# Reordering the steps of a two-layer attention pipeline on VectorE, GpSimd and the DMA queue

## The reference

```
x = x + tanh(g_xattn[0]) * L0_xattn(layernorm(x), ctx, ctx)     # similarity of probabilities, MLP of 1024 with gelu
x = x + tanh(g_ffn[0])   * L0_ffn(layernorm(x))                 # 256x256 product of values rounded to fp8
x = x + tanh(g_xattn[1]) * L1_xattn(layernorm(x), ctx, ctx, mask)   # 16 heads of 16, softmax
x = x + tanh(g_ffn[1])   * L1_ffn(layernorm(x))                 # dequantised weights, MLP of 1024 with silu
```

## Time and profile before

| what | us |
|---|---|
| median of 3 runs | 1618.51 |
| lowest and highest | 1613.52, 1624.93 |
| span of the profiled execution (first to last instruction) | 1614.4 |
| first stage and setup, up to the first instruction of the pipeline | 611 |

### The profile page before, as it was taken

The page is one execution under the profiler, slowest core; times in us unless marked ns, Lnnn a source line. Parts: engine busy times, 40 slices in busy tenths (PEclk is TensorE's granted clock), DMA queues, the critical chain, the costliest instruction groups (busy, mean ns, idle before and its releaser), DMA issues.

```text
span 1614.4 us, 42641 instructions
## 1 busy us (share of the span) xinstructions
PE 1486.5 (92%) x14155; PEld 1144.6 (71%) x14155; DVE 1316.4 (82%) x3187; ACT 1135.2 (70%) x2057; POOL 1034.7 (64%) x1392
## 2 busy tenths in 40 slices
PE   4999999999999972668999999999999999999997
PEld 2788888888888861435667676777777776777666
DVE  4698888888888875778988889898988889898742
ACT  7798888888888742355666666666666666676664
POOL 4588888888888744224556565665656566565445
PEclk9999999999999995588999999999999999999999
DMA  7322222322222002332223232232223232232200
GB/s 228 96 80 66 91 72 65 96 66 69 93 65 71 2 1 92 80 119 73 80 80 87 73 85 80 85 87 81 83 78 92 72 91 74 86 85 84 64 16 22
DMA packets 197690, 125.45 MB, mean 78 GB/s; under 512 B 44400, under 2 KB 196848, under 8 KB 197360
## 3 DMA queue, kind: packets, MB, share of 16 engines
q1 hardware_dynamic: 197616, 124.48, 26.2%
HBM read 92.69 MB, written 25.17 MB: 73 GB/s over the span
## 4 chain that ended last, share of the span: by engine, by line
PE 48%; SPq 4%; DVE 3%; issue 2%; DMA 2%; POOL 2%; ACT 1%; POOLq 0%
PE b_bank L1835 28%; PE b_bank L1910 7%; PE b_scoreT L1892 4%; PE b_score L1875 4%; PE b_bank L1843 2%; PE b_bank L1987 1%; SPq L1306 1%; DMA b_nmT<-b_nm 1%; DMA b_yT<-b_y 1%; SPq L1290 1%; DVE b_nm L1653 1%; SPq L1279 1%; PE b_bank L1925 1%; ACT b_E L1471 1%; SPq L1315 0%
## 5 line engine op out<-in xcount | busy, mean ns | idle before, releaser
L1471 ACT ACTIVATE b_E<-b_scoreT 128x1024 f32<-128x1024 f32 x256 | 262.2, 1024 | 152.5 <-PE b_scoreT L1892 151.3
L1653 DVE TENSOR_REDUCE b_nm<-b_score 128x4 bf16<-128x1024 f32 x256 | 313.3, 1224 | 54.6 <-PE b_score L1875 48.4
L31 ACT ACT_TABLE_LOAD x157 | 201.4, 1283 | 18.6 <-PEq L1059 15.2
L1835 PE MATMUL b_bank<-f,b_YT 128*128 128x256 bf16 x1536 | 190.3, 274 | 4.7 <-POOL b_YT L1404 4.6
L890 PE MATMUL bank<-hT,W1T 128*128 128x256 bf16 x1536 | 183.3, 273 | 2.4 <-DVE hT L706 1.7
L1835 PE MATMUL b_bank<-b_hT,f 128*128 128x256 bf16 x1536 | 183.4, 273 | 0.8 <-DVE X L1749 0.8
L890 PE MATMUL bank<-W2T,G 128*128 128x256 bf16 x1024 | 171.0, 272 | 6.7 <-DVE GT L780 6.2
L1835 PEld LDWEIGHTS b_bank<-f,b_YT 128*128 128x128 bf16 x1536 | 143.5, 98 | 39.7 <-issue 19.5
L1835 PEld LDWEIGHTS b_bank<-b_hT,f 128*128 128x128 bf16 x1536 | 147.7, 98 | 30.3 <-issue 12.6
L890 PEld LDWEIGHTS bank<-hT,W1T 128*128 128x128 bf16 x1536 | 148.0, 98 | 27.7 <-ACT G L549 4.0
L1388 POOL TENSOR_TENSOR b_v<-b_v,b_e 128x512 f32<-128x512 f32 x32 | 40.6, 1269 | 195.0 <-DVE b_e L1734 195.0
(11 more groups left out here) (222 smaller groups left out, 3524.8 us busy)
## 6 DMA issues: line engine op xcount, KB each, us to landing
b_Q<-q_dram SPq DMA_DIRECT2D x192, 64.0 KB, 2.6
b_K<-k_dram SPq DMA_DIRECT2D x192, 64.0 KB, 2.8
xin<-in_x SPq DMA_DIRECT2D x32, 256.0 KB, 3.2
ctxn<-in_ctx SPq DMA_DIRECT2D x32, 256.0 KB, 2.8
mask_in<-in_mask SPq DMA_DIRECT2D x32, 256.0 KB, 3.0
X<-in_x SPq DMA_DIRECT2D x32, 256.0 KB, 4.0
ctxt<-in_ctxT SPq DMA_DIRECT2D x32, 256.0 KB, 4.2
b_ctxt<-in_ctxT SPq DMA_DIRECT2D x32, 256.0 KB, 2.8
```

What stands on the lines that cost most here:

```text
L31: act.add_instruction(mybir.InstLoadActFuncSet(name=nc.get_next_instruction_name(), act_func_set_id=which, ins=[], outs=[]))
L1471: nc.scalar.activation(E[:, pair:pair + 2], scoreT_ps[:, :, :, :], ACT.Exp).then_inc(sig["E"], 1)
L1653: nc.vector.tensor_reduce(pair, score_ps[:, :, :, :], AX.X, ALU.max, negate=True).then_inc(sig["nm"], 1)
L1835: last = nc.tensor.matmul(out_tile, lhs(i, k), rhs(j, k), start=start and k == chunks[0] and (i, j) == TERMS[0], stop=stop and k == chunks ...
```

## The change

No instruction is added or removed; eight calls change place.

- VectorE: `scaled(n)` moves from the start of the iteration to just ahead of `binades(n)`. `statistics_2(f)` moves from behind `result` to ahead of `maxima(5)`. `mlp_normalised` moves from the start of an iteration to behind `maxima(6)` of the iteration before (so its batch is `o`, not `h`). `mask_bias` stays at its place but works one batch earlier (`q`, not `m`).
- GpSimd: `inverse_std_2(f)` comes before `silu_parts(h, 0)`, not after it; so both inverse deviations stand together.
- SyncE: `load_mask` comes before the spills and stacks, right behind `transpose_rounded`, and not behind `transpose_maxima`.

```diff
@@ -1327,14 +1327,13 @@
                     load_context()
                     transpose_rounded()
                 if q:
+                    load_mask()
                     spill_queries()
                     spill_keys()
                     stack_queries()
                     stack_keys()
                 if m:
                     transpose_maxima()
-                if q:
-                    load_mask()
                 if m:
                     row_of_maxima()
                 if w:
@@ -1440,11 +1439,10 @@
                     rounded()
                 if o:
                     inverse_std_3()
-                if h:
-                    silu_parts(h, 0)
                 if f:
                     inverse_std_2()
                 if h:
+                    silu_parts(h, 0)
                     silu_parts(h, 1)
                 if f:
                     context_parts()
@@ -1620,18 +1618,18 @@
                     nc.vector.tensor_tensor(xT[:, 1], whole_bank(BANK["xT"]), xT[:, 0], ALU.subtract).then_inc(sig["xlo"], 1)
 
                 def mask_bias():
-                    dve.wait_ge(sig[f"mask{m.parity}"], landed(m))
-                    if (due := done(m, back=2, per=NP)) is not None:
+                    dve.wait_ge(sig[f"mask{q.parity}"], landed(q))
+                    if (due := done(q, back=2, per=NP)) is not None:
                         dve.wait_ge(sig["scoreT_mm"], due)
-                    nc.vector.tensor_scalar(mb[m.parity][:, :, :], mask_in[:, :, :], 0.0, MINUS, ALU.is_equal,
+                    nc.vector.tensor_scalar(mb[q.parity][:, :, :], mask_in[:, :, :], 0.0, MINUS, ALU.is_equal,
                                             ALU.mult).then_inc(sig["mb"], 1)
 
                 def mlp_normalised():
-                    dve.wait_ge(sig["rs3"], done(h))
-                    if (due := done(h, back=1)) is not None:
+                    dve.wait_ge(sig["rs3"], done(o))
+                    if (due := done(o, back=1)) is not None:
                         dve.wait_ge(sig["hT_mm"], due)
                     for t in range(T):
-                        last = nc.vector.tensor_scalar(hn[:, t, :], Xb(h, t), mv3[:, t, 0:1], rh3[:, t:t + 1], ALU.subtract,
+                        last = nc.vector.tensor_scalar(hn[:, t, :], Xb(o, t), mv3[:, t, 0:1], rh3[:, t:t + 1], ALU.subtract,
                                                        ALU.mult)
                     last.then_inc(sig["hn"], 1)
 
@@ -1755,10 +1753,6 @@
 
                     dve.wait_ge(sig["b1_mm"], 1)
                     nc.vector.tensor_tensor(b1f[:, :], second["b1_raw"][:, :], b1_ps, ALU.add).then_inc(sig["b1f"], 1)
-                if h:
-                    mlp_normalised()
-                if n:
-                    scaled()
                 if o:
                     attended(0)
                 if m:
@@ -1782,6 +1776,7 @@
                 if h:
                     mlp_columns()
                 if n:
+                    scaled()
                     binades()
                 if f:
                     quantised_update()
@@ -1795,15 +1790,18 @@
                     keys_low()
                 if o:
                     attention_update()
+                if f:
+                    statistics_2()
                 if m:
                     maxima(5)
                     maxima(6)
+                if o:
+                    mlp_normalised()
                 if w:
                     result()
-                if f:
-                    statistics_2()
-                if m:
+                if q:
                     mask_bias()
+                if m:
                     maxima(7)
                 if f:
                     attention_normalised()
```

More of the change, by code:

```diff
@@ L1800, in iteration @@
                     maxima(6)
+                if o:
+                    mlp_normalised()
                 if w:
                     result()
-                if f:
-                    statistics_2()
+                if q:
+                    mask_bias()
                 if m:
-                    mask_bias()
                     maxima(7)
```

## The result

The changed kernel takes 1646.41 us (median of 4 runs, 1644.15 to 1652.79), the kernel before in the same comparison 1617.62: ratio 1.0177, 95% interval 1.0146 to 1.0208. It is slower, by 28.8 us; forecast were 26.5 us more and a median of 1645 us. The profiled execution has a span of 1644.8 us, 30.4 more than before.

The account below looks back on a forecast made before the run. TensorE, full from iteration 7 or 8, was taken as the bound, waiting on VectorE's chain at `scores(6)`. 30 - 3.5 + 0 = 26.5 us on the median of 1618.5 gave 1645 us, range 1633 to 1663.

Parts of the forecast that it names:

- 0.455 us to spare: Mean slack of VectorE's closed chain from `maxima(3)` to `maxima(5)`: 0.39 us in iteration 18, 0.52 in 17.
- the wait at `scores(6)`: TensorE waits there for `maxima(5)`: 1.33 us in iterations like 18, 1.20 in those like 17.
- The statistics: `statistics_2`, moved ahead of `maxima(5)`, adds 0.95 us to VectorE's chain; ends 0.95 and 1.01.
- The scaling: `scaled`, moved ahead of `binades`, adds 0.77 us to VectorE's chain; ends 0.65 and 1.06.
- Per iteration: Each steady iteration of the second stage, 7 to 31, gets 1.2 us longer.
- What came back: Iterations 8 to 14: the new delay gives DMA transfers more time, regaining 3.5 us; ends 0 and 4.
- The two waits for `b_on`: At `mlp_transposed`: of 5.29 us in iteration 6, 1.7 go; the 1.87 in iteration 7 go whole.
- The term of the start: Iterations 0 to 6: gains and losses sum to 0, give or take 4 us.
- the steady term: Iterations 7 to 31: 25 x 1.2 = 30 us more; ends 27 and 39.
- A (absorbed): Rival: the wait at `scores(6)` is absorbed, true slack 1.7 us; 1613 us, within 1%; chance 10%.
- B: Rival: faster by over 1%, as the start or the transfers win much more than is lost; chance 4%.
- C (the clock): Rival: TensorE's clock falls after the new wait, 32 us on top over 25 iterations, 1677 us; chance 5%.

Follow-up runs that it names:

- E6: Kernel before with one extra unused `bn_stats` on VectorE ahead of `maxima(4)`: 1617.97 us, ratio 1.0003.
- E7: Kernel before with four extra unused `bn_stats` on VectorE ahead of `maxima(4)`: 1641.19 us, ratio 1.0150.
- E8: Changed kernel with six extra unused `bn_stats` at the start of VectorE's iteration, ahead of `attended(0)`: 1651.49 us, ratio 1.0221 to the kernel before.
- E1: Kernel before with only `statistics_2` moved ahead of `maxima(5)`: 1627.6 us, ratio 1.0059.
- E2: Kernel before with only `scaled` moved to just ahead of `binades`: 1620.86 us, ratio 1.0017.
- E3: Changed kernel with `scaled` and `statistics_2` back in their old places: 1614.25 us, ratio 0.9986 to the kernel before.
- E12: Changed kernel with `scaled` and `binades` behind `quantised_update` instead of ahead of it: 1653.72 us, measured once.
- E4: As E3, but with `statistics_2` between `maxima(5)` and `maxima(6)`: 1613.7 us, ratio 0.9970 to the kernel before.

## Why the prediction was right

**The bound, and the place of the loss.** TensorE full, one score buffer, and a chain on VectorE from `maxima(3)` to `maxima(5)` with 0.455 us to spare: the wait at `scores(6)` appeared as forecast (1.20 us on the weight load, 0.92 between matmuls), at `scores(5)` as well (0.21 us between matmuls, in every second iteration), and nowhere else of weight. E6 and E7 show the slack, E8 that time ahead of the chain is worth nothing there, and the 0.44 us that E1 and E2 lack together show that both used the same slack.

One reading was a little off: VectorE did have idle time in the chain, 0.16 us in even iterations, in which the second instruction of `quantised_update` waits for the first. In odd ones that gap is 0.04 us, which is where the two values of the slack come from (kernel before, iterations 17 and 18):

```profile
1060.02 0.87 DVE L1658 SCALAR_TENSOR_TENSOR b_ob<-b_bank,scale_qk,fb_all 128x256 bf16<-128x256 f32 x2
...
1060.93 0.75 DVE L1662 SCALAR_TENSOR_TENSOR X<-b_ob,gate,X 128x512 bf16 x1
...
1087.96 0.87 DVE L1658 SCALAR_TENSOR_TENSOR b_ob<-b_bank,scale_qk,fb_all 128x256 bf16<-128x256 f32 x2
...
1088.98 0.75 DVE L1662 SCALAR_TENSOR_TENSOR X<-b_ob,gate,X 128x512 bf16 x1 [0.16 <-DVE b_ob L1658]
```

It costs the argument nothing, for VectorE can't use the gap for what stands behind it.

**The statistics: 0.95 us.** 1077.69 to 1078.65 and on to 1079.60 in the rows after: 0.96 and 0.95. Right.

**The scaling: 0.77 us forecast, 0.89 and 0.99 measured.** `columns` to `binades` was 0.40 us from start to start (1087.22 to 1087.62 in the trace before) and is 1.29 in iteration 17 (1070.80 to 1072.09) and 1.39 in 16 (1041.53 to 1042.92):

```profile
1087.22 0.22 DVE L1640 TENSOR_SCALAR b_tg<-b_rs,gate 128x2 f32<-128x2 f32 x1
...
1087.55 0.15 DVE L1643 SCALAR_TENSOR_TENSOR b_dn<-b_mv,b_tg 128x2 f32<-128x2 f32 x1
```

```profile
1041.53 0.22 DVE L1638 TENSOR_SCALAR b_tg<-b_rs,gate 128x2 f32<-128x2 f32 x1
...
1042.15 0.73 DVE L1714 TENSOR_SCALAR b_v<-X,mu,rsq 128x256 f32 x2
...
1042.92 0.43 DVE L1720 TENSOR_SCALAR b_e<-b_v 128x512 int32<-128x512 int32 x1
```

The first two rows are of the kernel before, the other three of the changed one. The pair takes 0.73 us, as I took it from iteration 0, and not the 1.02 that it took beside GpSimd; here the trace agrees with the rule of the Trainium skill ("SBUF — State Buffer", Reading the diagram), as it would with any slowing by GpSimd: GpSimd is idle at the new place, and no run tells a lock from another kind of contention. What I missed are the hand-overs: `binades` used to start 0.08 us before its predecessor's end, and `v` starts 0.04 us after it in iteration 17 and 0.13 after it in 16. 0.08 + 0.04 + 0.77 = 0.89, and 0.08 + 0.13 + 0.77 = 0.98.

**Per iteration: 1.2 forecast, 1.31 measured.** From `scores(3)` to `scores(6)` it was 10.28 us. Now it is 11.63 in iteration 17 and 11.83 in 18:

```profile
1098.30 0.38 PE L1873 MATMUL b_score<-b_K,b_Q 48*128 48x256 bf16 x4
...
1110.13 0.39 PE L1873 MATMUL b_score<-b_K,b_Q 48*128 48x256 bf16 x4 [0.92 <-DVE b_nm L1651]
```

That is 1.45 us more in the mean; I had 1.72 - 0.455 = 1.27, and the hand-overs are most of the difference. The forecast put this on 27.79 us, the length of iterations like 17; the floor is 27.71 (E3), so those had 0.08 us to lose too. 27.71 + 1.45 = 29.16, against 29.17 measured and 29.05 forecast. The term that was off is the scaling's; the mechanism was right.

**The output projection.** Not forecast: it waits for `b_ob` (0.30 us on the weight load, 0.08 between matmuls), since both products use one PSUM bank and the update now ends some 0.9 us later. It costs nothing of its own: the time is taken off the wait that follows, since `scores(6)` goes when VectorE's chain ends, and that chain doesn't wait for the output projection (its reader L1747 has no idle time before it). With the order of E12 the wait goes and the iteration gets no shorter.

**What came back: 3.5 us forecast.** From `binades` of iteration 8 (808.78) to that of 15 (1013.76) it is 204.98 us; the third row is that of 31, the other end of the 466.67 us above:

```profile
808.78 0.43 DVE L1720 TENSOR_SCALAR b_e<-b_v 128x512 int32<-128x512 int32 x1
...
1013.76 0.43 DVE L1720 TENSOR_SCALAR b_e<-b_v 128x512 int32<-128x512 int32 x1
...
1480.43 0.43 DVE L1720 TENSOR_SCALAR b_e<-b_v 128x512 int32<-128x512 int32 x1
```

Seven iterations of 29.17 are 204.2, so 0.8 us are left of what was 4.0; 3.2 came back. Half of my reason for it was wrong. Of the waits for the row of maxima one of 0.2 us is left, as is to be expected if SyncE's chain has more time (no run separates this). But `quantised_product` still waits for `yT`, in iterations 10 and 11 by more than before:

```profile
866.96 0.61 PE L1923 MATMUL b_bank<-wf,b_yT 128*128 128x256 bf16 x4 [1.26 <-DMA b_yT<-b_y]
...
896.78 0.61 PE L1923 MATMUL b_bank<-wf,b_yT 128*128 128x256 bf16 x4 [1.27 <-DMA b_yT<-b_y]
```

Those iterations are 29.70 and 29.68 us long, only 0.5 above the others: the wait lies inside the stretch that VectorE's chain sets, and the longer chain hides 0.7 us of it. What I had called time given to the transfers is, for `yT`, one wait in the shadow of another.

**The start and the end.** From iteration 0 to 8 it is 4.3 us longer than before, of which 1.1 is iteration 7, counted among the 25; for the rest, 3.2 us, I had said 0, give or take 4. The two waits for `b_on` shrank as forecast (5.29 to 3.77 us, and 1.87 to nothing). Against this, TensorE waits 4.3 us more for the maxima and 1.6 more for `yT` in this stretch. That last part isn't tied to the scaling or the statistics: in iteration 5 TensorE waits 4.51 us for `yT` where it was 2.89, but E3, which has neither of the two moves, waits 4.41 there, and its stretch is 3.0 us longer as well. Over the twelve experiments the stretch takes from 191.8 to 199.9 us, each in one execution, and what sets these transfers stays open. Behind iteration 31 nothing is lost, though 1.2 us of my sum were for iteration 31 itself.

**The sum, and what was luck.** The spans differ by 30.4 us and I had said 26.5. By the stretches: 4.3 against 1.2 from iteration 0 to 8 (the 1.2 for iteration 7), 5.9 against 4.9 from 8 to 15, 20.9 against 19.2 from 15 to 31, and -0.7 against 1.2 for what lies around them. The term of the start was 3 us too low, and the steady term too low by 0.1 us an iteration. The medians differ by 28.8, only 2.3 from the forecast; that they come closer than the spans is scatter, since the median of the kernel before alone moved by 0.9 us with its fourth run. Slower by some 25 to 30 us was earned by the mechanism, a hit within 2 us was not.

**The rivals.** A (absorbed) falls with E6 and E7, and E1 to E3 give 0.44 us for the slack that I read as 0.455. B has no ground: all that the other moves give is E3's 0.14%, and its interval holds no change. C (the clock) did not occur: granted 1.00 with a wait of 1.20 us in every iteration, and the values' products at 1084.23 take 1.93 us, 3 us after it. What the Trainium skill ("TensorE: Matmul & The Clock Gate", A second HAM failure mode: psum-queue depth-cycling) tells of another kernel did not happen with one such wait in 29 us.

## What to carry to other kernels

In a software pipeline whose main engine is full, look on each helper for the stretch between the last thing that it gets from the main engine and the next that it must give back; only work inside such a stretch counts, against that stretch's own slack, and two moves into the same stretch share the slack once. While the main engine is full, idle time elsewhere on the helper is worth nothing, but an idle gap directly behind a hand-back (here between `maxima(5)` and `maxima(6)`) takes a step for free: the same six instructions cost 0.52 us an iteration on one side of one reduce and nothing on the other. The version to keep is E4, or E3, from which its time can't be told.

## What the runs showed beside

Instructions on VectorE that follow each other without a wait overlap by about 0.08 us here; the pair of scalings, put between two that did, came with a gap of 0.04 or 0.13 us ahead of it and 0.04 behind it, and so cost 0.89 to 0.99 us for a duration of 0.73. And a wait of about 1 us, once in each 29 us, left TensorE at 2.4 GHz: the granted clock is 1.00 in the windows from iteration 7 to 31 (779.87 to 1480.43 us).
